# A decoder of two layers: keys and values of the context projected in a stage of their own, half products stacked in 64 rows per head, the diagonal of maxima made by GpSimd

## What is computed

```
xn = layer_norm(x)                         # layer 1 also normalises the context
q = xn @ Wq + bq      # 112 x 256
k = context @ Wk + bk # 375 x 256
v = context @ Wv + bv # 375 x 256
attn = softmax(q_h @ k_h.T / 4)            # 112 x 375 for each head h
x = x + concat_h(attn @ v_h) (@ Wo + bo in layer 0; + nothing in layer 1)
```

## Time and profile before

| | us |
|---|---|
| median of 3 runs (3871.74 to 3872.47) | 3871.93 |
| the profiled execution | 3868.77 |
| its span | 3867.0 |
| cross attention 0, first to last instruction | 542 to 1309 |
| cross attention 1, first to last instruction | 2458 to 3333 |
| PE busy over the span | 3016.1 (78%) |
| DVE, ACT, POOL busy | 1709.9, 1316.2, 905.7 |
| moved by DMA | 234.68 MB, mean 61 GB/s |

### The profile page before, as it was taken

How to read it: one execution, slowest core, us unless ns; L and a number is a source line. 1 busy time by engine, 2 the same in 40 slices (tenths; PEclk the granted TensorE clock), 3 DMA queues, 4 the chain that set the end, 5 groups by cost and what they waited for, 6 DMA issues and landing times. The chain is left out here.

```text
span 3867.0 us, 59553 instructions
## 1 busy us (share of the span) xinstructions
PE 3016.1 (78%) x19704; PEld 2381.5 (62%) x19704; DVE 1709.9 (44%) x3313; ACT 1316.2 (34%) x2657; POOL 905.7 (23%) x934
## 2 busy tenths in 40 slices
PE   4999929999999820999993588788888888709980
PEld 2666618777778710888882355466676667608870
DVE  2444467666667532000003444465655556502323
ACT  1222245555555300333330222344444445302220
POOL 0000004433334150000004100232323333160015
PEclk7999959999999755999996789899999999759995
DMA  4000000000000233565552000000000000035653
GB/s 109 1 1 0 0 9 13 14 13 16 13 14 13 96 102 97 170 199 190 182 199 88 19 0 0 12 13 14 10 13 10 13 7 13 1 92 182 202 171 113
DMA packets 174569, 234.68 MB, mean 61 GB/s; under 512 B 25184, under 2 KB 141376, under 8 KB 174384
## 3 DMA queue, kind: packets, MB, share of 16 engines
q1 hardware_dynamic: 156496, 184.23, 15.4%
q0 software_dynamic: 17888, 47.73, 3.7%
HBM read 186.04 MB, written 45.88 MB: 60 GB/s over the span
## 5 line engine op out<-in xcount | busy, mean ns | idle before, releaser
L1214 POOL TENSOR_TENSOR x_qH<-x_q_high,head_mask 128x448 fp32r<-128x448 f32 x256 | 277.0, 1082 | 1580.3 <-DVE x_q_low L1271 1246.4
L1284 DVE TENSOR_REDUCE x_neg_max<-banks 112x2 f32<-112x750 f32 x512 | 456.3, 933 | 259.7 <-PE banks L998 259.6
L1156 ACT ACTIVATE x_probT<-banks 125x448 f32<-125x448 f32 x768 | 417.1, 543 | 420.4 <-PE banks L1018 412.0
L1014 PE MATMUL banks<-x_qH,x_kS 128*125 128x448 f32 x768 | 383.5, 499 | 34.9 <-issue 32.4
L1734 PE MATMUL banks<-f_xT,f_w 128*128 128x256 f32 x1680 | 386.2, 385 | 17.6 <-DMA f_w<-in_L_ffn_w 12.9
L1746 PE MATMUL banks<-f_w,f_hT 128*128 128x256 f32 x1680 | 374.2, 379 | 0.0
L1734 PEld LDWEIGHTS banks<-f_xT,f_w 128*128 128x128 f32 x1680 | 319.6, 192 | 76.3 <-issue 23.2
L1746 PEld LDWEIGHTS banks<-f_w,f_hT 128*128 128x128 f32 x1680 | 313.9, 190 | 39.9
L1018 PE MATMUL banks<-x_diag,x_ones 112*125 112x448 f32 x768 | 288.9, 376 | 0.0
L1016 PE MATMUL banks<-x_qL,x_kS 128*125 128x448 f32 x768 | 288.2, 375 | 0.0
L970 PE MATMUL banks<-x_ctxT,x_wk 128*128 128x375 f32 x512 | 203.7, 522 | 83.0 <-DVE x_o L1302 79.9
(11 more groups left out here) (271 smaller groups left out, 4989.0 us busy)
## 6 DMA issues: line engine op xcount, KB each, us to landing
f_w<-in_L_ffn_w SPq DMA_DIRECT2D x70, 1024.0 KB, 8.3
f_w<-in_L_ffn_w SPq DMA_DIRECT2D x70, 512.0 KB, 5.0
f_x_slots<-slot_x SPq DMA_DIRECT2D x70, 256.0 KB, 6.0
slot_y<-f_y POOLq DMA_DIRECT2D x70, 256.0 KB, 5.5
f_ctx_rows<-in_ctx SPq DMA_DIRECT2D x32, 281.2 KB
x_cnat<-in_ctx SPq DMA_DIRECT2D x32, 281.2 KB
slot_x<-f_zero SPq DMA_DIRECT2D x10, 896.0 KB, 11.6
x_ctxT<-in_ctx_T SPq DMA_DIRECT2D x32, 187.5 KB
```

The source lines that it names most:

```text
L1014: pe.matmul(to, kS[:, r, q, keys], qH[:, r, heads, :].rearrange("p h t -> p (h t)"), start=True, stop=False)
L1156: act.activation(probT[:, u % 2, c].rearrange("k h t -> k (h t)"), ST[i % 2][0:KB, 0:HU * T], ACT.Exp).then_inc(exp_done, 1)
L1214: pool.tensor_tensor(qH[:, r, to, :], wide(q_high[:, q:q + 1, :], 1, HU), mask, ALU.mult).then_inc(qH_ready, 1)
L1284: dve.tensor_reduce(mx[:, u % 2, 2 * pair:2 * pair + 2], psum[0:T, 2 * pair:2 * pair + 2, 0:NKV], AX_X, ALU.max, negate=True).then_inc(max ...
```

## The change: what it does

Two new stages, `project_context(e, 0)` and `(e, 1)`, run ahead of the cross attentions. For each of 32 batches they load the context (and normalise and transpose it in layer 1), compute k and v as before, cut k in halves on ACT and DVE, and store both in DRAM: `k_halves` (770 KB a batch: 2 head parities x 2 halves x 128 rows x 376) and `v_rows` (768 KB a batch, 125 partitions x 1536). Weights and biases are reordered once so that a row group holds one element of all heads.

The cross attention now loads both back, batch by batch. Heads are taken in pairs; each head has 64 partitions of its own: 32 rows of k (16 high, 16 low), twice, against 32 rows of the query's high half and 32 of its low half. The duplication is made by the load: `wide(parts[...], 0, 2)` puts a leading dimension of 2 with stride 0 on the source, so that one transfer of 64 partitions reads 32 rows twice. Of the query (`q_halves`) the same: it is stored in DRAM after the cut and loaded by four transfers of 32 partitions that read 16 rows twice. Per batch these are four key transfers of 64 x 6016 B, four query transfers of 32 x 3584 B, one load of the values of 125 x 6144 B, and one query store of 128 x 4 x 448 B, all on SP's queue, in the order keys, query, values, store.

A step becomes one matmul of 448 columns (ones x diag) and two of 224 (a pair of heads each, all four half products in one pass). The scores run two units ahead instead of one, spread over two steps; q is computed two batches ahead, its matmuls halved (8 PE instructions). `make_diag` moves from DVE to GpSimd, with 4 buffers; GpSimd's masks go.

```diff
+        env.k_halves = nc.dram_tensor("k_halves", [B, 2, 2, P, NKV + 1], F32, kind="Internal").ap()
+        env.v_rows = nc.dram_tensor("v_rows", [B, KB, NJ * XH * P // XU], F32, kind="Internal").ap()
+        env.q_halves = nc.dram_tensor("q_halves", [2, 2, 2, P, T], F32, kind="Internal").ap()
...
-        stages = [self_attention, lambda e: cross_attention(e, 0), lambda e: experts(e, 0),
-                  gated_attention, lambda e: cross_attention(e, 1), lambda e: experts(e, 1)]
+        stages = [self_attention, lambda e: project_context(e, 0), lambda e: cross_attention(e, 0),
+                  lambda e: experts(e, 0), gated_attention, lambda e: project_context(e, 1),
+                  lambda e: cross_attention(e, 1), lambda e: experts(e, 1)]
...
+def project_context(e, layer):
...
+                def load(b, i, r):
+                    if layer == 0:
+                        sp.wait_ge(v2_ps, ONE + least(i * 2 + r - 1))
+                        sp.dma_start(ctxT[:, r, 0, :], d["ctx_T"][0:P, bass.ds(b, 1), :].rearrange(
+                            "c b k -> c (b k)")).then_inc(ctx_loaded[r], 16)
+                        sp.dma_start(ctxT[0:C1, r, 1, :], d["ctx_T"][P:DC, bass.ds(b, 1), :].rearrange(
+                            "c b k -> c (b k)")).then_inc(ctx_loaded[r], 16)
+                    else:
+                        sp.wait_ge(cT_ps, ONE + least(i * 4 + 2 * r - 2))
+                        sp.dma_start(cnat[:, r, :, 0:DC], d["ctx_768"][bass.ds(b, 1)].rearrange(
+                            "b (j p) c -> p (b j) c", p=KB)).then_inc(ctx_loaded[r], 16)
+                def store(b, i, r):
+                    sp.wait_ge(k_low, ONE + i * 4 + 2 * r + 2)
+                    sp.dma_start(e.k_halves[bass.ds(b, 1)].rearrange("b h l p n -> p (b h l) n"),
+                                 halves[:, r].rearrange("p h l n -> p (h l) n").bitcast(F32)).then_inc(k_stored[r], 16)
+                    sp.wait_ge(v01_ready, ONE + i * 2 + r + 1)
+                    sp.wait_ge(v2_ready, ONE + i * 2 + r + 1)
+                    sp.dma_start(e.v_rows[bass.ds(b, 1)].rearrange("b p n -> p (b n)"),
+                                 v[:, r].rearrange("p c h e -> p (c h e)")).then_inc(v_stored[r], 16)
+                for r in range(2):
+                    load(r, 0, r)
+                with sp.Fori(1, B // 2) as i:
+                    for r in range(2):
+                        store(i * 2 + r - 2, i - 1, r)
+                        load(i * 2 + r, i, r)
+                for r in range(2):
...
+                    for m in range(KD):
+                        pe.wait_ge(k_low, ONE + least(i * 4 + 2 * r + m - 1))
+                        for k in range(2):
+                            last = pe.matmul(KEYS[m][:, 0:NKV], wk[:, k, m, :], ctxT[:, r, k, :],
+                                             start=(k == 0), stop=(k == 1))
+                        last.then_inc(k_ps, 1)
+                    for cs, to, done, ready in ((range(2), V01[r], v01_ps, v01_ready),
+                                                (range(2, NJ), V2[r], v2_ps, v2_ready)):
+                        pe.wait_ge(ready, ONE + least(i * 2 + r - 1))
+                        for c in cs:
+                            at = c % 2 * D
+                            for k in range(2):
+                                last = pe.matmul(to[0:KB, at:at + D], ctxT[:, r, k, c * KB:(c + 1) * KB],
+                                                 a.wv[:, k, :], start=(k == 0), stop=(k == 1))
+                        last.then_inc(done, 1)
...
+                    for m in range(KD):
+                        act.wait_ge(k_ps, ONE + i * 4 + 2 * r + m + 1)
+                        if type(i) is not int:
+                            act.wait_ge(k_stored[r], i * 16)
+                        act.activation(halves[:, r, m, 0, 0:NKV], KEYS[m][:, 0:NKV], ACT.Identity,
+                                       bias=a.bk[:, m:m + 1]).then_inc(k_high, 1)
...
+    PAIRS = H // 2
     F32R = mybir.dt.float32r
-    if layer == 0:
-        AT = {"xT": 1, "q": 2, "k0": 4, "back": 5, "k1": 7, "v2": 8, "oT": 9, "v01": 10, "y": 11}
-        LOW = {"k0": 7, "k1": 10}
-    else:
-        AT = {"cT0": 1, "cT1": 2, "xT": 3, "k0": 4, "q": 5, "back": 6, "k1": 7, "v2": 8, "v01": 10}
-        LOW = {"k0": 7, "k1": 10}
+    AHEAD = 2
+    RING = 4
+    AT = {"xT": 1, "q": 2, "back": 4, "oT": 7, "y": 8}
...
+                def load_keys(g, s):
+                    b = g * GROUP + s
+                    r = s % 2
+                    sp.wait_ge(st_ps, ONE + since(g, NU * NJ, SS * (s - 1)))
+                    parts = e.k_halves[bass.ds(b, 1)].rearrange("b h l (d p) n -> (b h) (l d) (p n)", d=HD)
+                    for half in range(2):
+                        pairs = slice(half * PAIRS // 2, (half + 1) * PAIRS // 2)
+                        keys = slice(pairs.start * (NKV + 1), pairs.stop * (NKV + 1))
+                        for h in range(2):
+                            sp.dma_start(kP[h * HALF:(h + 1) * HALF, r, pairs, :].bitcast(F32),
+                                         wide(parts[h:h + 1, :, keys], 0, 2)).then_inc(k_loaded[half][r], 16)
+                def load_values(g, s):
+                    b = g * GROUP + s
+                    r = s % 2
+                    sp.wait_ge(pv_ps, ONE + since(g, NU, SU * (s - 1)))
+                    sp.dma_start(v[:, r].rearrange("p c h e -> p (c h e)"),
+                                 e.v_rows[bass.ds(b, 1)].rearrange("b p n -> p (b n)")).then_inc(v_loaded[r], 16)
+                def store_query(g, s):
+                    r = s % 2
+                    sp.wait_ge(q_cut, ONE + g * (2 * GROUP) + 2 * s + 2)
+                    sp.dma_start(e.q_halves[r].rearrange("h l p t -> p (h l) t"),
+                                 q_halves[:, r].rearrange("p h l t -> p (h l) t").bitcast(F32)).then_inc(q_stored[r], 16)
+                def load_query(g, s):
+                    r = s % 2
+                    sp.wait_ge(q_stored[r], g * (8 * GROUP) + 16 * (s // 2 + 1))
+                    parts = e.q_halves[r].rearrange("h l (d p) t -> h l d (p t)", d=HD)
+                    for h in range(2):
+                        for l in range(2):
+                            at = h * HALF + 2 * l * HD
+                            sp.dma_start(qP[at:at + 2 * HD, r, h].rearrange("q p t -> q (p t)").bitcast(F32),
+                                         wide(parts[h, l:l + 1], 0, 2)).then_inc(q_loaded[r], 16)
+                def group(g, is_first, last):
                     for s in range(GROUP):
-                        b = g * GROUP + s
-                        r = s % 2
-                        if layer == 0:
-                            sp.wait_ge(v_ps, ONE + g * (2 * GROUP) + (2 * (s - 1) if s >= 2 else 0))
-                            sp.dma_start(ctxT[:, r, 0, :], d["ctx_T"][0:P, bass.ds(b, 1), :].rearrange(
-                                "c b k -> c (b k)")).then_inc(ctx_loaded[r], 16)
-                            sp.dma_start(ctxT[0:C1, r, 1, :], d["ctx_T"][P:DC, bass.ds(b, 1), :].rearrange(
-                                "c b k -> c (b k)")).then_inc(ctx_loaded[r], 16)
-                        else:
-                            sp.wait_ge(cT_ps, ONE + g * (2 * GROUP) + (2 * (s - 1) if s >= 2 else 0))
-                            sp.dma_start(cnat[:, r, :, 0:DC], d["ctx_768"][bass.ds(b, 1)].rearrange(
-                                "b (j p) c -> p (b j) c", p=KB)).then_inc(ctx_loaded[r], 16)
+                        if s < GROUP - 1 or not last:
...
-                    if pair == 0:
-                        pe.wait_ge(qH_ready, ONE + g * (SU * GROUP) + SU * s + q + 1)
-                        pe.wait_ge(kS_low, ONE + g * (2 * GROUP) + 2 * s + q // 2 + 1)
+                    if pair == 0 and q % 2 == 0:
+                        pe.wait_ge(k_loaded[q // 2][r], g * (16 * GROUP) + 32 * (s // 2 + 1))
+                    if pair == 0 and q == 0:
+                        pe.wait_ge(q_loaded[r], g * (32 * GROUP) + 64 * (s // 2 + 1))
                     pe.wait_ge(max_done, ONE + since(g, 2 * NU, n - 1))
                     for k in range(2):
-                        last = pe.matmul(bank[2 * pair + k][0:T, 0:NKV + 1], qH[:, r, q * HU + 2 * pair + k, :],
-                                         kS[:, r, q, :], start=True, stop=True)
+                        last = pe.matmul(bank[2 * pair + k][0:T, 0:NKV + 1], qP[:, r, k, 2 * q + pair, :],
+                                         kP[:, r, 2 * q + pair, :], start=True, stop=True)
                     last.then_inc(s_ps, 1)
...
-                        pe.wait_ge(qL_ready, ONE + g * (SU * GROUP) + SU * s + q + 1)
                         pe.wait_ge(diag_ready, ONE + g * NU + u + 1)
                     pe.wait_ge(exp_done, ONE + since(g, NU * NJ, i - 1))
                     to = ST[i % 2][0:KB, 0:HU * T]
                     keys = slice(c * KB, (c + 1) * KB)
```

(86 more changed lines are left out.)

508 lines of the change are left out of this document (261 added, 247 removed).

## The result

The changed kernel takes 6285.18 us (4 runs, 6279.60 to 6290.53) against 3872.20: ratio 1.623, 95% interval 1.620 to 1.626. The forecast was 6100, with a range of 5650 to 6750.

A forecast was written before the change was run, and what follows sets the result against it. Key and query loads confined to two DMA engines were to bound the cross attentions: 3868.8 + 825 + 680 (cross attentions) + 728 (projections) = 6102, forecast 6100 us, range 5650 to 6750.

The forecast's parts named there:

- The mechanism: Cross attention loads: 125 partitions get five DMA engines, so key and query sources leading with 2 get two.
- Rate: Cross attention transfers: one DMA engine carries 420/16 = 26.3 GB/s.
- The batch: Cross attention: latency 2.6, keys 29.3, query 8.7 and second half 8.6 us, 49.2 us in layer 0, 48.0 in layer 1.
- the second half: Cross attention, PE's work after the wait: 6.2 us at 2.4 GHz plus 2.4 for starting at half clock, 8.6 us.
- the key load: Cross attention: keys of a batch, 770 KB on each of the busiest two engines, take 29.3 us.
- TensorE's work: Cross attention: PE needs 14.1 us a batch in layer 0 and 12.9 in layer 1, hidden behind the transfers.
- The 224-column matmul: Cross attention step: each takes 0.11 us, between half of 0.205 and 0.187, so 0.43 us a step.
- Diagonals: Cross attention: four a batch on GpSimd at 1.03 us, 4.1 us in place of 8.2 for masks, hidden below 14 us.
- Projections: New projection stages: 10 and 11.5 us a batch plus 20 us to start and drain, 340 + 388 = +728 us.
- the floor: Projection stages: work on engines 0 to 4 (value store, key store, context) takes 9.0 and 10.7 us a batch.
- Rival 1: Cross attention: copies do not confine the loads, all 16 engines work, TensorE bounds; 3811 us; chance 0.08.
- rival 2: Cross attention: loads spread, but SP's issues and other 1 MB delay the query, 16.5 and 15.5 us a batch; 4029 us; chance 0.07.

The follow-up runs named there:

- e1: The changed kernel with key and query loads each split by copy into two transfers whose source leads with 32 or 16 rows: 4138.85 us, ratio 1.069.
- e2: The changed kernel with only the key loads split by copy, the query still leading with 2: 4589.94 us.
- e4: The changed kernel with key and query loads leading with a zero-stride 4 over half as many rows, same bytes: 5043.34 us.
- e3: The changed kernel with key loads leading with 2 at a nonzero stride, the second copy holding the other half of the columns: 6189.18 us.
- e9: e7 with SP's order changed to keys of units 0 and 1, query, keys of units 2 and 3: 3679.79 us, ratio 0.951 to before.
- e8: e7 with the diagonals made by VectorE again, not GpSimd: 3872.72 us, ratio 0.987 to before.
- e11: The changed kernel with values stored and loaded as 128 rows, three of zeros, in place of 125: 6182.41 us.
- e12: e10 with SP issuing the context load ahead of the stores in layer 1's projection stage: 3605.70 us, ratio 0.916 to before.
- e6: e1 with the copies inside the row dimension, 6 issues of SP a batch in place of 16, same bytes: 3988.51 us, ratio 1.015 to before.
- e7: e6 with values stored and loaded as 128 rows in place of 125: 3874.49 us, ratio 0.987 to before.
- e10: e9 with VectorE normalising the next batch's context ahead in layer 1's projection stage: 3718.52 us, ratio 0.961 to before.

## Why the prediction was right

**The mechanism.** A step from one row, five engines for 125 partitions, to two engines for a leading 2 carried nearly all of the forecast. e1, e2 and e4 show it by number, and e3 that a stride of zero under the keys is worth at most 1.3 of the 52.8 us.

**Rate.** Taken 26.3 GB/s for one engine; 26.5 in the trace, 25.9 by the fit over e4.

**The batch.** Forecast 49.2 / 48.0 us, measured 52.8 / 51.8; 30 times that difference is 108 of the 115 us that cross attention 0 is over its 1592, and 114 of the 113 over 1555 in layer 1. In the batch shown, which takes 52.0, the second half, taken 8.6 us, is 8.1. The term that was mis-sized is the key load: latency, keys and query were to take 40.6 us and take 43.9. Its first 9 us run at 33 GB/s, with the share already at 0.13, and only then at 53 (windows above); 9 x (1 - 33/53) is 3.4 us, the size of the difference. Nothing in the rows of before could show that. Layer 1 was forecast 1.2 us a batch below layer 0 and is 1.0 below.

**TensorE's work.** It lies hidden here, but e9 lays it open: 14.2 and 13.2 us a batch, forecast 14.1 and 12.9. The 224-column matmul, taken at 0.11 us between the bounds of half of 0.205 and 0.187, is 0.105. On PE's timeline after the change the two of 224 columns start at 1511.65 and the next score at 1511.86, so the pair takes the 0.21 us of the one of 448 ahead of it (1511.44 to 1511.65), as in the earlier trace rows:

```profile
1511.44 0.37 PE L1182 MATMUL banks<-x_diag,x_ones 112*125 112x448 f32 x1
1511.65 0.38 PE L1184 MATMUL banks<-x_qP,x_kP 128*125 128x224 f32 x2
1511.86 0.50 PE L1168 MATMUL banks<-x_kP,x_qP 128*112 128x376 f32 x2
```

**Diagonals.** 0.94 us on GpSimd for 1.03 taken, hidden (e8).

**Projections.** Forecast 340 and 388, measured 305 and 403 (397 and 6 us of statistics). Layer 0 runs at 9.05 us a batch, the floor of 9.0 that the busiest engines set; the 1 us of waits that I put on top of it did not come, and start and end took some 15 of the 20 us. Layer 1 runs at 11.9 where 11.5 was taken and 10.7 was the floor, but the floor is not what holds it: without the five-engine store it still takes 10.2 us a batch (344 us, e11), and 6.7 once the next context is normalised ahead and its load no longer stands behind the stores (237 us, e12).

**Sum.** 115 + 113 us too little in the cross attentions, 35 too much in projection 0, 15 too little in projection 1, and 14 us saved up to projection 0, nearly all in the setup, which the forecast had named as some us: +194. Against that stand 13 us that before spends and the sum did not take off: 2 and 2 us up to the next stage's first load, and the 9 us of statistics ahead of cross attention 1, which are part of the new stage now. That leaves the 181 between 6102 and the profiled 6282.77. The misses of 115 and 113 us have one cause and add up; that the other terms pull the other way, by 47 us together, is luck.

**Rivals.** Rival 1 supposed that with all engines TensorE would bound at once, 3811 us. e1 gives it the engines and lands at 4139, nearer rival 2's 4029, with 19.0 / 18.2 us a batch for its 16.5 / 15.5 and twice its issues; that SP's issues delay the query, its mechanism, fits e6. Rival 1's cross attentions are reached in e9, once TensorE bounds them: 479 and 443 us for its 476 and 438, from key load to next stage.

## What to carry to other kernels

Before putting a broadcast into a transfer, look at the outermost dimension of its source: a leading 2 left two engines of sixteen at work here, with 64 and 32 partitions on the other side, and with the same copies one dimension further in (e6) the share stood at 0.87 while keys and query came in (1211 to 1213 us). Then count the issues ahead of the transfer that is waited for, and issue first what the first consumer needs: here that order alone gave 163 us in the two stages, 4% of e7. A load queued behind a store inherits the store's waits; moving a consumer earlier without its load made the stage slower (e10), both together made it nearly a third shorter (e12: 237 us for 344).

## What the runs showed of the hardware, unexpected

- Key loads on two engines start at 30 to 36 GB/s and reach 53 only after some 9 us, at the same share of 0.13. It is so in the prologue of cross attention 0 too, with TensorE at a granted clock of 0.50 and 39% busy (836 to 848 us: 31 GB/s). It does not hang on SP's issuing: in the batch whose four key transfers were issued from 2411.23 on in 2.26 us, it lasts until some 2423 us (first window below), and in the prologue 10 us beyond the last of the four. A busy TensorE at that clock does not bring it by itself either (second window, the end of a query load: 52 GB/s). The cause is open.

```profile
2414.00:2423.00 9.00, 5.76 (x79) 4.89 (x77) 4.04 (x8) 3.25 (x8) 2.55 (x3) 1.00 0.13 37
2456.00:2460.00 4.00, 4.00 (x28) 3.61 (x32) 1.88 (x2) 1.42 (x3) 0.66 (x1) 0.50 0.13 52
```

- An issue on SP, 0.3 to 0.6 us in e9, takes 5 us where it stands behind key loads that two engines carry: 20.15 us for four query loads above, 2.50 for four of the same size in e9. SP is blocked for that time.
- Chips differ by 1.7% on the same kernel (before: 3869.0 to 3935.4 us), so only runs against before on the same chip were compared in ratios.
